# Moving an expert's column of sums through PSUM by ScalarE, with the inner layer in two banks instead of four

## What is computed

```
scores = softmax(xt @ Wr)                      # [4096, 8]
G, idx = top_k(scores.T, 1024)                 # per expert
h   = gelu(xt[idx] @ W1 + b1)                  # [8, 1024, 512]
X_e = h @ W2 + b2                              # [8, 1024, 128]
out = zeros.at[idx].add(G[..., None] * X_e)
x   = x + tanh(g_ffn[1]) * out
```

## Time and profile before

| what | value |
|---|---|
| median of the runs | 961.47 us |
| the profiled execution's own time | 967.42 us |
| its span | 965.7 us |
| mean granted TensorE clock over the span | 0.911 |
| TensorE busy | 772.4 us, 80% |
| VectorE busy | 689.2 us, 71% |
| ScalarE busy | 494.7 us, 51% |
| GpSimd busy | 614.8 us, 64% |
| 32 adds of L1777 | 1.22 us each, 823.8 to 960.7 us |

### The profile page before, as it was taken

The page is one execution under the profiler, slowest core; times in us unless marked ns, Lnnn a source line. Parts: engine busy times, 40 slices in busy tenths (PEclk is TensorE's granted clock), DMA queues, the critical chain, the costliest instruction groups (busy, mean ns, idle before and its releaser), DMA issues. The chain is left out here.

```text
span 965.7 us, 30722 instructions
## 1 busy us (share of the span) xinstructions
PE 772.4 (80%) x9843; PEld 590.3 (61%) x9843; DVE 689.2 (71%) x2096; ACT 494.7 (51%) x1719; POOL 614.8 (64%) x1114
## 2 busy tenths in 40 slices
PE   3999999999957998369999999999930278888770
PEld 2777777777743666247777778778720146657560
DVE  3788888888866664157888888888869756775334
ACT  2777777777740212047877877777710032342320
POOL 4888666666643676467877877777410266777772
PEclk9999999999977999579999999999965579999995
DMA  6111222222113333134333443343200225665567
GB/s 173 60 64 63 85 76 73 73 73 73 72 60 94 101 103 99 46 99 132 122 111 125 138 129 113 126 138 122 78 15 0 65 49 139 180 183 160 163 187 217
DMA packets 98743, 100.83 MB, mean 104 GB/s; under 512 B 24510, under 2 KB 76076, under 8 KB 98658
## 3 DMA queue, kind: packets, MB, share of 16 engines
q1 hardware_dynamic: 88306, 88.25, 29.4%
q0 software_dynamic: 6656, 9.66, 3.7%
q10 hardware_dynamic: 3696, 1.84, 0.7%
HBM read 60.84 MB, written 44.17 MB: 109 GB/s over the span
## 5 line engine op out<-in xcount | busy, mean ns | idle before, releaser
L558 ACT ACTIVATE P<-bank,mx 128x120 f32<-128x120 f32 x1024 | 278.1, 436 | 12.9 <-DVE mx L849 12.4
L460 PE MATMUL bank<-ident,P 128*120 128x128 f32 x1024 | 166.4, 285 | 12.2 <-ACT P L558 9.1
L849 DVE TENSOR_REDUCE mx<-bank 128x4 f32<-128x480 f32 x256 | 150.3, 649 | 18.2 <-PE bank L447 15.3
L460 PEld LDWEIGHTS bank<-ident,P 128*120 128x120 f32 x1024 | 106.0, 137 | 58.0 <-issue 29.1
L1695 POOL DMA_INDIRECT xg<-token_rows,tokens x64 | 66.3, 1036 | 71.0 <-DVE tokens L1749 52.1
L476 PE MATMUL bank<-PT,Vb 120*32 120x128 f32 x2048 | 105.9, 279 | 0.0
L476 PE MATMUL bank<-PT,headcols 120*32 120x128 f32 x2048 | 102.8, 273 | 0.0
L437 PE MATMUL bank<-bp,identr 128*128 128x480 f32 x256 | 87.3, 427 | 0.0
L1705 POOL DMA_INDIRECT expert_sums<-y,sum_rows x64 | 72.2, 1129 | 23.4 <-issue 18.9
L660 POOL TENSOR_TENSOR Qm<-qf,qmask 128x512 f32<-128x512 f32 x64 | 67.4, 1054 | 27.5 <-ACT qf L542 26.7
L624 POOL TENSOR_SCALAR rs<-mv 128x1 f32<-128x1 f32 x128 | 28.9, 226 | 84.6 <-DVE mv L831 84.3
(11 more groups left out here) (245 smaller groups left out, 1819.3 us busy)
## 6 DMA issues: line engine op xcount, KB each, us to landing
expert_sums<-zeros SPq DMA_DIRECT2D x32, 512.0 KB, 3.4
choice_rows<-zeros SPq DMA_DIRECT2D x32, 384.0 KB, 2.4
yrows<-choice_rows SPq DMA_DIRECT2D x32, 384.0 KB, 3.2
XT<-expert_sums SPq DMA_DIRECT2D x16, 512.0 KB, 6.6
XS<-expert_sums SPq DMA_DIRECT2D x16, 512.0 KB, 6.1
w<-in_w13T SPq DMA_DIRECT2D x8, 704.0 KB, 4.1
token_rows<-payload SPq DMA_DIRECT2D x32, 128.0 KB, 1.7
ctx<-in_ctxT SPq DMA_DIRECT2D x64, 60.0 KB, 1.9
```

The costliest lines, as they stand in the source:

```text
L460: mm = nc.tensor.transpose(TB[r % 2][0:KV, S * j:S * j + S], t.P[:, r, j, :], t.ident[:])
L558: e = nc.scalar.activation(t.P[:, r, j, :], heads(SC[r])[:, j, :], ACT.Exp, bias=t.mx[:, G * r + j:G * r + j + 1], scale=-1.0)
L849: ve.tensor_reduce(t.mx[:, G * r:G * r + G], heads(SC[r]), AX.X, ALU.min).then_inc(ev.mins, 1)
```

## The change

The inner layer gets two banks, `HB[c % 2]`, in place of four. The two others, `COL`, take the columns. ScalarE copies an eighth of a column (4 batches, 128x512) from SBUF into one of them (`move_column`, two eighths for each quarter q), and VectorE adds it from there to X (`add_column`). Both work on the column of expert e-2 while expert e is computed, and their four parts are spread over the expert. The last column (expert 7) is still added straight from SBUF. `summed` now counts eighths, and SyncE may load a quarter again once ScalarE has moved it (`col_moved`). Two semaphores of the attention blocks, for the cleared tables of the two layers, become one (`t.cleared`), of which the second layer waits for twice the count. Cut to its core:

```diff
-        ev.cleared = sem("choices_cleared")
-        ev.sums_cleared = sem("sums_cleared")
+        t.cleared = sem("tables_cleared")
...
-            sp.wait_ge(ev.cleared if L == 0 else ev.sums_cleared, 16 * B)
+            sp.wait_ge(t.cleared, 16 * B * (L + 1))
...
-    HB, Y, TB = ps[0:4], ps[4:6], ps[6:8]
+    HB, COL, Y, TB = ps[0:2], ps[2:4], ps[4:6], ps[6:8]
+    CB = B // 8
...
-                    later(sp, ev.summed, PARTS * (e - 2) + q + 1)
+                    later(sp, ev.col_moved, 8 * (e - 2) + 2 * q + 2)
...
-                sp.wait_ge(ev.summed, PARTS * (E1 - 1) + q + 1)
+                sp.wait_ge(ev.summed, 8 * (E1 - 1) + q + 1)
...
-                    later(pe, ev.gelu, 8 * e + 4 * s + c - 3)
-                    nc.tensor.matmul(HB[c][:, :], t.w1x[:, e % 2, 128 * c:128 * c + 128],
+                    later(pe, ev.gelu, 8 * e + 4 * s + c - 1)
+                    nc.tensor.matmul(HB[c % 2][:, :], t.w1x[:, e % 2, 128 * c:128 * c + 128],
...
-                    nc.scalar.activation(t.ge[:, s, c, :], HB[c][:, :], ACT.Gelu,
+                    nc.scalar.activation(t.ge[:, s, c, :], HB[c % 2][:, :], ACT.Gelu,
...
+            def move_column(e, q):
+                if e < 0:
+                    return
+                act.wait_ge(ev.sums[q], 16 * (e + 1))
+                for h in range(2):
+                    n = 8 * e + 2 * q + h
+                    later(act, ev.summed, n - 1)
+                    part = slice(CB * (2 * q + h), CB * (2 * q + h) + CB)
+                    nc.scalar.activation(COL[h][:, :], columns(e)[:, part, :].rearrange("p b d -> p (b d)"),
+                                         ACT.Copy).then_inc(ev.col_moved, 1)
             copy(0)
             for e in range(E1):
+                move_column(e - 2, 0)
                 gelu(e, 0)
+                move_column(e - 2, 1)
                 gelu(e, 1)
+                move_column(e - 2, 2)
                 if e + 1 < E1:
                     copy(e + 1)
+                move_column(e - 2, 3)
+            for q in range(PARTS):
+                move_column(E1 - 2, q)
...
+            def add_column(e, q):
+                if e < 0:
+                    return
+                for h in range(2):
+                    n = 8 * e + 2 * q + h
+                    part = slice(CB * (2 * q + h), CB * (2 * q + h) + CB)
+                    dve.wait_ge(ev.col_moved, n + 1)
+                    later(dve, ev.summed, n - 7)
+                    ve.tensor_tensor(t.X[:, part, :], COL[h][:, :].rearrange("p (b d) -> p b d", b=CB),
+                                     t.X[:, part, :], ALU.add).then_inc(ev.summed, 1)
...
             for e in range(E1):
                 gates(e)
+                add_column(e - 2, 0)
+                add_column(e - 2, 1)
                 if e == 0:
                     make_list(2)
                     scale(0, 0)
...
                 if e >= 1:
                     scale(e, 0)
+                add_column(e - 2, 2)
                 scale(e, 1)
-                if 1 <= e < E1 - 2:
-                    add_sums(e - 1)
-            for e in range(E1 - 3, E1):
-                add_sums(e)
+                add_column(e - 2, 3)
+            for q in range(PARTS):
+                add_column(E1 - 2, q)
+            add_last_column()
```

More of the change, by code:

```diff
@@ L356, in clear_choices @@
             def clear_choices(b):
-                sp.dma_start(row(d.choices, b), t.zeros[:]).then_inc(ev.cleared, 16)
+                sp.dma_start(row(d.choices, b), t.zeros[:]).then_inc(t.cleared, 16)
             def load_bias(b, u):
@@ L365, in clear_sums @@
                 sp.dma_start(row(d.sums, b).rearrange("p (x c) -> p x c", x=2),
-                             t.zeros[:, 0:4 * D].unsqueeze(1).broadcast_to([S, 2, 4 * D])).then_inc(ev.sums_cleared, 16)
+                             t.zeros[:, 0:4 * D].unsqueeze(1).broadcast_to([S, 2, 4 * D])).then_inc(t.cleared, 16)
             def load_choices(b, u):
@@ L1543, in experts1_block @@
     ev.sums = [sem(f"moe_sums_loaded{q}") for q in range(PARTS)]
+    ev.col_moved = sem("moe_column_moved")
     ev.summed = sem("moe_summed")
@@ L1770, in scale, with add_last_column @@
                                  ALU.mult).then_inc(ev.scaled, 1)
-            def add_sums(e):
+            def add_column(e, q):
[8 more added lines that the diff above has]
+                                     t.X[:, part, :], ALU.add).then_inc(ev.summed, 1)
+            def add_last_column():
+                e = E1 - 1
                 for q in range(PARTS):
@@ L1775, in add_sums @@
                     dve.wait_ge(ev.sums[q], 16 * (e + 1))
-                    later(dve, ev.summed, PARTS * (e - 1) + q + 1)
+                    dve.wait_ge(ev.summed, 8 * (e - 1) + 2 * q + 2)
                     ve.tensor_tensor(t.X[:, part, :], t.X[:, part, :], columns(e)[:, part, :], ALU.add).then_inc(ev.summed, 1)
```

## The result

| | before | after |
|---|---|---|
| median of 20 runs each | 964.46 us (958.55 to 971.79) | 970.87 us (965.21 to 974.38) |
| ratio, 95% interval | | 1.0058 [1.0036, 1.0079] |
| profiled execution, its own time | 967.42 us | 971.8 us |
| its span | 965.7 us | 970.1 us |
| ScalarE busy; GpSimd busy | 494.7; 614.8 us | 521.1; 601.4 us |

The change makes the kernel slower by 0.6%. The profiled executions stand 4.4 us apart, and that is the difference explained here. Of the 9 us between 961.8 and 970.87, 3.0 are the base: the three runs shown before had 961.47, the twenty have 964.46.

A forecast was written before the change was run, and what follows sets the result against it. GpSimd's indirect DMA queue, then TensorE's loop, bound the second experts. turn(7) +3.3, clock -2.7, hidden(7) +3.5, place(7) -4.1 netted 0.0; 961.5 plus 0.3 for waits gave 961.8 us, range 958 to 965.5, 8 in 10 within 952.5 to 968.

The forecast's parts named there:

- What falls away: GpSimd's stalls beside seven columns' adds vanish: 8.9 us on the way to gather(7), 4.1 us in place(7).
- The prices: ScalarE's copy of 128x512 from SBUF to PSUM takes 0.60 us, VectorE's add from a bank 0.69.
- The order of waits: From expert 3, the first GELU waits behind adds and copies until 3.45 us; the list's pick comes at 11.2 instead of 8.9.
- TensorE's arrival at turn(7): Delays summed over experts 0 to 6, written as +9.25 us, move it from 908.68 to 918.2.
- The clock: TensorE's granted clock: 2.7 us gained as the pause before turn(7) ends; no lower clock priced behind the new stops.
- rows 9: Profile rows around 798.60, cited against a lower clock: 2.95 us of pause, then a stretch at full clock.
- rival 2: Slower: new stops in hidden lower TensorE's clock in experts 3 to 7; 971 us, or 966 for two or three; chance 0.15.
- the two banks in experts 0 and 1: Inner layer with two banks alone makes TensorE wait for GELUs there: +0.4 us with the slow start.
- The range: Forecast's own range 958 to 965.5 us; the range of 8 in 10 was 952.5 to 968.
- Rival 1: Faster: copies and adds overlap the GELUs, TensorE's loop is not lengthened; 13 us less, 948.5, half-way 955; chance 0.19.
- Rival 3: GpSimd's stalls stay despite adding from banks, so place(7) keeps its 4.1 us: 965.9 us; chance 0.07.

The follow-up runs named there:

- filler kernel: The changed kernel with two more 128x512 matmuls, results unread, ahead of the third block of experts 3 to 7; 0.9972 of the kernel before.
- the GELU first: The changed kernel with gelu(e, 0) moved ahead of move_column(e - 2, 0) on ScalarE; 1.0020 of the kernel before.
- reordered kernel: The changed kernel with GELUs ahead of their copies and the adds placed elsewhere in VectorE's list; 0.9947 of the kernel before at 967 us, 1.0159 to 1.0196 at 1036.

## Why the prediction was wrong, point by point

- **What falls away: right.** 8.9 us and 4.1 us of GpSimd's stalls were to go. GpSimd's loss after 805 us sank by 12.6 us, place(7) by 3.9. (The 13 rows counted add up to 21.5 us, so 9.0 rather than 8.9.) The pause before turn(7) and its low clock went too: turn(7) and out(6,1) take 925.75 - 921.30 = 4.45 us.
- **The prices: right.** A copy takes 0.60 us, an add from a bank 0.69 with 0.60 from start to start.
- **The order of waits: right.** GELU 3.39 us after hidden's start (forecast 3.45), pick at 854.03 - 842.75 = 11.3 (11.2), expert 3 21.94 us (21.8), expert 6 up to turn(7) 13.87 (14.0). The third block waited 2.23 us.
- **TensorE's arrival at turn(7).** The terms listed add up to 9.55, not the 9.25 written; the 918.2 carried on has 9.5. It came at 921.30, +12.6.
- **The clock: this step failed.** The sum had no lower clock behind the new stops. "rows 9 do not agree, and no row here has stops at banks" was taken as a reason for 0, and rival 2, which priced it at 966 to 971, got 0.15. place(7) was forecast for 934.87 + 4.1 = 938.97 and came at 943.25, 4.3 us later. Of these the clock is 3.7: 1.4 in expert 4, 1.1 in expert 5 and 1.2 from hidden(7) on, by which the filler kernel, at the full clock, is shorter. The rest is mainly a second term that was too small, the two banks in experts 0 and 1: forecast +0.4, measured 823.31 - 822.23 = +1.1, with 7.66 us for a hidden of 7.03, as with the two banks alone. One stretch with full clock behind a single stop of 2.95 us was weak evidence, all the more as a stop of 3.36 us in expert 4 had shown 0.85. In the trace after, the very place of the earlier trace rows has a stop of 3.18 us and the lower clock behind it (TensorE in order of time):

```profile
797.75 0.27 PE L1608 MATMUL bank<-counts_hi,oh 128*128 128x129 bf16 x1 [3.18 <-DVE oh L1753]
...
798.19 2.02 PE L1641 MATMUL bank<-w2x,ge 128*128 128x128 f32 x8
```

The same eight products took 1.11 us before (798.84 to 799.95). The Trainium skill, "TensorE: Matmul & The Clock Gate", section "A second HAM failure mode: psum-queue depth-cycling", tells of this, and the trace after agrees, with 0.91, 0.91 and 0.94 in the three stretches. The fall is no certainty at each stop, though: it did not come in experts 3 and 6, nor behind five of the six stops of 1.9 us with the GELU first. The place of the earlier trace rows had the full clock again in the filler kernel (its eight products at 799.34 took 1.11 us), whose fillers start only at expert 3, so it changes from one execution to the next.
- **The range.** Its upper end, 968, left the second rival out at about 970. The base of 961.47 was 3.0 us low as well, and no fault of the mechanism: from 964.46 the same sum gives 964.8. With that rival at the weight that a stop in every expert deserves, it would have reached 972.
- **Rival 1** came near the reordered kernel: pick 8.0 us after hidden's start (839.07 to 847.07), 0.9947. turn(7) comes 5.8 us earlier in the stage than before the change, where the rival has 6.3. But hidden(7) then takes 12.2 us instead of 6.9, as the load of column 5 is late, so only 5 to 6 of its 13 us are had.
- **Rival 3 was half a truth not seen:** the stall is not on or off, it is longer or shorter with the add.

## What to carry to other kernels

A helper put into an engine's ordered list delays what stands behind it by all that it waits for, so place it behind the work that feeds the bound engine; here the same copies and adds gave 1.006 or 0.995 of the time by their place alone, where the kernel before takes 964 to 967 us. Where a change gives TensorE a regular stop of some 2 us, price the granted clock behind it as well, from every stop in the trace and not from the one that suits, and keep both outcomes in the range: here stops of 1.9 to 2.2 us were followed by the lower clock in some experts and not in others. If an engine is held up by another's instruction, try shorter instructions in another place before rerouting the data.

## What the runs showed of the hardware

- **GpSimd's indirect DMA instructions are held up beside VectorE's operations with two SBUF operands, and the more the longer one such operation is:** up to 1.97 us beside adds of 128x1024 (1.14 us from start to start), 1.50 beside 128x512 (0.61), 1.04 beside 128x256 (0.34), against 0.97 alone and beside adds from a bank (846.05 in the trace after). The Trainium skill, "SBUF — State Buffer", section "Who interferes with whom", gives the two-input form as one that contends with reads, and infers that descriptor generation is spared. These rows contradict the inference, if what these instructions do on GpSimd is the generation of descriptors.
- **ScalarE copies 128x512 from SBUF to a bank in 0.60 us**, as fast as from a bank to SBUF.
- **Regular stops of TensorE at a bank can bring the lower clock:** with one of 2.23 us per expert, eight matmuls took 5.48 us instead of 3.95 in one expert and 3.95 in another; with two matmuls put into each stop the clock was 1.00 in all of them.
- **The same kernel took 967 and 968 us on two chips and 1032 to 1037 on three others,** with the attention loops alike. The cause is not known.
